# A fused decoder layer: the cross-head scores in blocks of two tokens (64x32 pieces of TensorE's array), picked from two candidates in place of four

## What is computed

```python
q = (query @ Wq.T + bq).reshape(b, s, 16, 64)      # query: x after sublayer 1
k = (key @ Wk.T + bk).reshape(b, s, 16, 64)        # key, value: ctx
scores = jnp.einsum('bshd,bsgd->bshg', q, k) / 8   # head h against head g of the SAME token
attn = softmax(scores, axis=-1)
out = jnp.einsum('bshg,bsgd->bshd', attn, v)
```

## Time and profile before

| | |
|---|---|
| three runs | 489.27, 483.74, 486.50 us; median 486.5 |
| the profiled execution | 491.25 us, of which 489.4 us from the first to the last instruction |
| TensorE's mean granted clock | 0.972 |
| busy | PE 426.4 us, PEld 364.3, DVE 342.6, ACT 242.7, POOL 146.5 |

### The profile page before, as it was taken

The page is one execution under the profiler, slowest core; times in us unless marked ns, Lnnn a source line. Parts: engine busy times, 40 slices in busy tenths (PEclk is TensorE's granted clock), DMA queues, the critical chain, the costliest instruction groups (busy, mean ns, idle before and its releaser), DMA issues.

```text
span 489.4 us, 12635 instructions
## 1 busy us (share of the span) xinstructions
PE 426.4 (87%) x4788; PEld 364.3 (74%) x4788; DVE 342.6 (70%) x751; ACT 242.7 (50%) x828; POOL 146.5 (30%) x218
## 2 busy tenths in 40 slices
PE   8779699999898977999898977899898989999793
PEld 7568577778787866778787866778787877778683
DVE  2543788884958794884958794875958798967534
ACT  3584646534565353534565353643565364645431
POOL 5030425050330533050321542151321543512121
PEclk9889899999999997999999997999999999999998
DMA  8800201110100112010100112010100110101002
GB/s 214 308 2 1 50 7 45 55 40 2 29 23 12 40 26 70 13 38 1 30 23 12 39 27 68 17 35 5 29 18 16 37 29 21 43 6 43 21 1 64
DMA packets 43588, 19.10 MB, mean 39 GB/s; under 512 B 36544, under 2 KB 40896, under 8 KB 43536
## 3 DMA queue, kind: packets, MB, share of 16 engines
q1 hardware_dynamic: 42688, 16.88, 12.5%
q0 software_dynamic: 560, 1.38, 1.1%
q10 hardware_dynamic: 288, 0.07, 0.1%
HBM read 8.88 MB, written 1.05 MB: 20 GB/s over the span
## 4 chain that ended last, share of the span: by engine, by line
PE 61%; DVE 21%; issue 9%; ACT 4%; POOL 3%; DMA 2%; SPq 0%; POOLq 0%; DVEq 0%; ACTq 0%
PE ps L1018 7%; PE ps L923 6%; PE ps L1096 6%; PE ps L1071 6%; PE ps L948 6%; DVE pt L660 4%; DVE qt L705 4%; PE ps L1196 3%; PE ps L903 3%; PE ps L972 3%; PE ps L905 3%; PE ps L1135 3%; PE ps L904 3%; DVE ot L643 3%; DVE neg_max L712 3%
## 5 line engine op out<-in xcount | busy, mean ns | idle before, releaser
L496 ACT ACTIVATE p<-ps,neg_max 128x128 f32<-128x128 f32 x256 | 91.1, 414 | 66.9 <-DVE neg_max L712 66.9
L386 POOL TENSOR_TENSOR p<-p,row_inv 128x1024 f32<-128x1024 f32 x32 | 60.4, 1898 | 104.1 <-DVE row_inv L794 97.1
L489 ACT ACTIVATE pt<-ps 128x512 f32<-128x512 f32 x64 | 34.9, 607 | 66.6 <-PE ps L1018 66.5
L496 ACT ACTIVATION_READ_ACCUMULATOR p<-ps,neg_max 128x1 f32 x256 | 65.3, 255 | 0.0
L705 DVE TENSOR_TENSOR qt<-ps,bq 64x256 f32<-64x256 f32 x128 | 53.4, 417 | 7.5 <-PE ps L1135 5.8
L1018 PE MATMUL ps<-ident,p 128*128 128x128 f32 x256 | 37.2, 300 | 10.3 <-issue 7.1
L712 DVE TENSOR_REDUCE neg_max<-ps 128x4 f32<-128x512 f32 x64 | 42.1, 683 | 0.2 <-PE ps L1122 0.2
L1018 PEld LDWEIGHTS ps<-ident,p 128*128 128x128 f32 x256 | 31.7, 154 | 13.8 <-issue 11.5
L1135 PE MATMUL ps<-x1t,wq 128*128 128x128 f32 x256 | 36.5, 286 | 5.8 <-DVE pt L660 3.0
L948 PE MATMUL ps<-wo,ot 128*128 128x128 f32 x256 | 32.3, 279 | 10.0 <-DVE ot L643 10.0
L1135 PEld LDWEIGHTS ps<-x1t,wq 128*128 128x128 f32 x256 | 31.1, 191 | 11.8 <-DVE pt L660 8.1
(11 more groups left out here) (138 smaller groups left out, 891.7 us busy)
## 6 DMA issues: line engine op xcount, KB each, us to landing
v<-v2s SPq DMA_DIRECT2D x256, 32.0 KB
xg<-x_t SPq DMA_DIRECT2D x4, 256.0 KB, 2.7
pt<-w_qk SPq DMA_DIRECT2D x4, 256.0 KB, 7.2
cg<-ctx_t SPq DMA_DIRECT2D x4, 256.0 KB, 3.1
wo<-w_o SPq DMA_DIRECT2D x2, 512.0 KB, 9.1
out<-x2b SPq DMA_DIRECT2D x4, 256.0 KB, 2.3
xres<-x_nat SPq DMA_DIRECT2D x15, 64.0 KB, 1.7
bv_row<-b_v POOLq DMA_DIRECT2D x1, 512.0 KB, 10.7
```

What stands on the lines that cost most here:

```text
L386: nc.gpsimd.tensor_tensor(ph, ph, row_inv[:, 8 * half:8 * half + 8].unsqueeze(2).to_broadcast([T, 8, T]), ALU.mult).then_inc(p_ready, 1)
L496: last = nc.scalar.activation(p[:, hd * T:(hd + 1) * T], bank(S_BANK[q])[:, pos * T:(pos + 1) * T], ACT.Exp, bias=neg_max[:, hd:hd + 1], a ...
```

## The change

It cuts the tokens of a product from four to two. The constant `JB` = 2 is new. Each round i now has two blocks `ja` of two tokens for each half: 64 products of 64x32 in a step in place of 32 of 64x64. A block's stationary and moving operands are 32 columns each, and its result goes to partitions 64*pp + 32*ja on, so that a product occupies an eighth of the array (rows 64*ih, columns 64*pp + 32*ja), given as `tile_position`. The products' results fill the first 32 of every 64 columns of the PSUM banks. The pick takes two candidates: one `tensor_scalar` and one `scalar_tensor_tensor`. `own_j` has two columns and is made for `% JB` on the host.

```diff
-        own_j = sb("own_j", [128, J])
+        own_j = sb("own_j", [128, JB])
...
-                    scores = bank(S2, BANK, 2).rearrange("p (i j g) -> p i j g", i=IH * K, j=J)
+                    scores = bank(S2, BANK, 2).rearrange("p (i x j g) -> p i x j g", i=IH * K, x=2, j=JB)[:, :, 0]
                     own = s2v
                     nc.vector.tensor_scalar(own, scores[:, :, 0], own_j[:, 0:1], None, ALU.mult).then_inc(own_picked, 1)
-                    for j in range(1, J):
-
-                        dve.wait_ge(own_picked, (J - 1) * s - (J - 1) + j)
-                        nc.vector.scalar_tensor_tensor(out=own, in0=scores[:, :, j], scalar=own_j[:, j:j + 1], in1=own,
-                                                       op0=ALU.mult, op1=ALU.add).then_inc(own_picked if j < J - 1 else s2_ready, 1)
+                    dve.wait_ge(own_picked, s)
+                    nc.vector.scalar_tensor_tensor(out=own, in0=scores[:, :, 1], scalar=own_j[:, 1:2], in1=own,
+                                                   op0=ALU.mult, op1=ALU.add).then_inc(s2_ready, 1)
                     max2(s + 1)
...
                     for i in range(K * 2):
                         k, pp = i // 2, i % 2
-                        first = ((phase - 1) % GB * K * 2 + i) * J * H
-                        for ih in range(IH):
-                            rows = slice(64 * ih, 64 * ih + 64)
-                            last = nc.tensor.matmul(bank(S2 + ih)[64 * pp:64 * pp + 64, k * 64:(k + 1) * 64],
-                                                    qt2[rows, i * J * H:(i + 1) * J * H], kb[rows, first:first + J * H], start=True, stop=True)
+                        for ja in range(J // JB):
+                            own = i * J * H + ja * JB * H
+                            first = (phase - 1) % GB * HALF * H + own
+                            below = 64 * pp + 32 * ja
+                            for ih in range(IH):
+                                rows = slice(64 * ih, 64 * ih + 64)
+                                last = nc.tensor.matmul(bank(S2 + ih)[below:below + 32, k * 64:k * 64 + 32],
+                                                        qt2[rows, own:own + JB * H], kb[rows, first:first + JB * H], start=True, stop=True,
+                                                        tile_position=(64 * ih, below))
                     last.then_inc(mm_s2, 1)
```

More of the change, by code:

```diff
@@ L39 @@
 IH, J, K = 2, 4, 8
+JB = 2
 FH, FL = 512, 64
@@ L1269 @@
     mask[np.arange(128), np.arange(128) // H] = 1.0
-    own_j = np.zeros((128, J), np.float32)
-    own_j[np.arange(128), np.arange(128) // H % J] = 1.0
+    own_j = np.zeros((128, JB), np.float32)
+    own_j[np.arange(128), np.arange(128) // H % JB] = 1.0
     x = np.asarray(x)
```

## The result

Four runs of the changed kernel have a median of 499.81 us (496.76 to 502.47), four of the kernel before 487.88 (483.74 to 489.52): a ratio (of the means) of 1.0256, with an interval of [1.0164, 1.0347]. The forecast was 485.7 us, no change, and its range ended at 497.0. The profiled execution of after took 500.1 us, its span is 498.3, against 491.25 and 489.4 before; TensorE's mean granted clock is 0.976 (before 0.972).

What follows compares the result with a forecast made beforehand. TensorE was taken as the bound from the output projection 948 through the next one. Products 0, step 1 -0.4, pick -0.9 and instructions +0.5 sum to -0.8 us, giving 485.7 us from the median 486.5; 8-in-10 range 481.0 to 497.0.

Steps and rivals of the forecast that it cites:

- Where the change stands: TensorE's cross-head scores lie on the path in every step, VectorE's pick in hardly any.
- The products: count and price: Scores in each step: 128 records at 6.8 ns plus 0.22 us fixed make 1.09 us, no change.
- four pieces streaming 32 columns: Scores: the array work per product halves on four pieces, 6.8 ns per record, paying exactly for twice the products.
- the row of the starts: Scores: narrow windows show four records starting within 0.03 us, at most one each 7.5 ns, 1.18 us per set.
- the pace is per record, not per column: Rival: a record takes about 13.6 ns whatever its size, scores 1.96 us, kernel 499.6 us; chance 0.22.
- More instructions: TensorE's 2,048 added instructions make late fetches at the loop's branch likelier: +0.5 us (0 to +7.1).
- the fetches bind: Rival: both idle times at the branch double, +7.1 us, kernel 492.3 us; chance 0.05.
- The pick: VectorE's shorter pick gains 0.23 us from step 15 into 16 and 0.66 behind step 16: -0.9 us (0 to -2.0).
- in an ordinary step: VectorE waits for others soon behind the pick, so its 1.0 us saved per step counts zero.
- Step 1: Its scores, 1.99 us at the lower clock, were to change by -0.4 us (0 to -0.9).
- The sum: Whole kernel: 0 - 0.4 - 0.9 + 0.5 = -0.8 us, 485.7 us from the median of 486.5.
- signs that the forecast had named: Scores of 1.4 us or more, 0.8 or less, releaserless TensorE idle inside or behind them, or steps a microsecond shorter.

Runs made afterwards that it cites:

- e7_half: Changed kernel with only the first block of each round, 32 products of 64x32 (half of the scores left out): 480.65 us, 0.9856 of the kernel before.
- e13_one_pass: Changed kernel with qt2 and kb in bfloat16, each product one load and one matmul: 486.14 us, 0.9977 of the kernel before.
- e2_products_only: Changed kernel with its 64 products of 64x32 but four picks again, two of them times zero: 499.9 us, 1.0242 of the kernel before.
- e1_pick_only: Kernel before with its 32 products of 64x64, but VectorE picks only two of four candidates: 485.15 us against 487.45, 0.9951.
- e5_moving16: Changed kernel with 16 moving columns in place of 32, same number of instructions: 501.15 us, 1.0264 of the kernel before.
- e6_moving64: Changed kernel with 64 moving columns in place of 32, same number of instructions: 502.42 us, 1.0289 of the kernel before.
- e8_twice: Kernel before with each of its 64x64 products made twice, 128 records per set of scores: 505.69 us, 1.0357 of the kernel before.
- e9_after_shift80: Changed kernel with 20 short matmuls behind TensorE's warm-up, later instructions 80 places further on: 504.88 us, 1.032 of the kernel before.
- e11_after_shift128: Changed kernel with 32 short matmuls behind TensorE's warm-up, later instructions 128 places further on: 507.56 us, 1.0427 of the kernel before.
- e3_after_shift128: Changed kernel with 128 increments of an unused semaphore at the head of TensorE's program: 515.26 us, 1.057 of the kernel before.
- e10_before_shift80: Kernel before with 20 short matmuls behind TensorE's warm-up, 80 instructions: 493.2 us, 1.0097 of the kernel before.
- e4_before_shift128: Kernel before with 128 increments of an unused semaphore at the head of TensorE's program: 505.87 us, 1.0379 of the kernel before.

## Why the prediction was wrong, point by point

- **Where the change stands** was right: the scores lie on the path in every step, the pick in hardly any.
- **"The products: count and price"** is the step that failed. The count, 128 records, was right. The price of 6.8 ns per record came from "four pieces streaming 32 columns" and from the row of the starts. But the runs with 16 and 32 columns show that streaming is no bound there, and a burst of four starts says nothing of a run of 128. The windows of after, L1198 alone, show how a burst misleads (the first figure behind x is the matmul records in flight):

```profile
134.56:134.73 0.17, 0.17 (x32) 0.17 (x33) 1.00 0.44 107
134.73:134.80 0.07, 0.07 (x32) 0.07 (x18) 1.00 0.30 62
```

  The first 32 records start within 0.17 us, some 5.2 ns apart, faster even than forecast. In the next 0.07 us none is added. From then on the trace has a product each 16.7 ns, which is 8.4 ns per record, with a pause of some 0.2 us near the 90th; over the block it is 1.44/128 = 11.3 ns. In the blocks of 1.64 to 1.76 us the pauses add up to 0.3 to 0.45 us. Over the 13 steps they come to 3.4 of the 6.0 us. Their cause is open: no run here moves them by design, and e7_half and e13_one_pass, with half of the instructions, have none in step 4. The forecast 1.09 us were 1.44 to 1.76, +6.0 us in 13 steps and some 0.7 of the 1.74 in steps 6 and 10, where the sum had 0.
- **The rival "the pace is per record, not per column"** had the mechanism for the changed kernel and was dear by a seventh of its price: 11.7 ns per further record and not 13.6. Its point of decision, 10 ns, was passed. That its total, 499.6 us, lies 0.2 from the measured 499.81 is luck: it had 1.96 us per set of scores, which took 1.44 to 1.76, and no stops, which made up for it. It also had the 13.6 ns of the kernel before as a pace of records, and e7_half's 0.69 us for as many records say that there it was not. It was weighed at 0.22 because the earlier trace rows seemed to speak for streaming: at the lower clock the same block took 1.99 us. That is a reading of 64x64 products, whose size counts (1.09 us against e7_half's 0.69 for as many records); it doesn't carry over to 64x32.
- **"More instructions"** was far too small: +0.5 us, for the branches alone. Behind steps 4, 8 and 12 it is +4.25 us, in the scores of step 1 a stop of 2.28 us, and at the branches 8.2 us of idle time for 7.1. This is the second step that failed. "Nothing in the chain before shows one in a straight stretch" was true and no argument: before, a set of scores used up 128 instructions in 1.1 us, now it uses up 256, as many as a packet holds. The rival "the fetches bind" looked for it at the branches, where little of it was.
- **"The pick"**: -0.9 us forecast. 0.23 and 0.66 us were right in kind: line 1095 of step 16 and line 929 behind it wait no longer, and the 1.28 us for ScalarE's gelu stay, as the timeline of after shows:

```profile
438.24 1.95 PE L1095 MATMUL ps<-wo,ot 128*128 128x128 f32 x16
...
463.64 1.16 PE L971 MATMUL ps<-wdn,qt 128*128 128x128 f32 x8 [1.28 <-ACT qt L482]
465.35 0.44 PE L929 MATMUL ps<-ident,p 128*128 128x128 f32 x2
```

  These places gave 0.49 and 0.79 us, and 0.6 more came by the wait for `x` (line 773), which the step "in an ordinary step" had put at zero. -1.9 us in all.
- **Step 1** gave nothing of the -0.4 us: its scores took 2.11 us more, for the stop of 2.28 us inside them. In e2_products_only, which has no stop there, they take 0.16 us less than before.
- **The sum**: -0.8 was forecast. With the measured terms it is +6.0 + 1.7 + 4.3 + 3.0 - 2.2 - 1.9 - 2.1 = +8.8, the 8.9 us between the two spans but for rounding. The medians are 11.9 us apart, with an interval that holds both.

Two of the signs that the forecast had named for its being wrong came together: scores of 1.4 us or more, and idle times without a releaser inside and behind them.

No version here with the whole computation is faster than the kernel before. e1_pick_only and e7_half leave out part of it, e13_one_pass changes its numbers.

## What to carry to other kernels

The long row of tiny products here was priced by its instructions: count loads and matmuls, and take the pace from a run as long as the one that is planned, never from a burst of four. Cutting a product into two halves can pay only as long as the array's work is the bound; where it no longer is, the halves cost together more than the whole did (1.44 us for 1.09). And whoever puts as many instructions as one fetch brings into less time than a fetch takes should look for idle time without a releaser, not in that place but a little behind it.

## What the runs showed of the hardware

**Fetches of instructions.** 0.82 MB in 50 packets are 16.4 KB each; the Trainium skill (Runtime: NRT & Kernel Launch, Instruction fetch mechanics) says that they come in blocks of 16 KiB, 256 instructions, and the packets' size agrees. Such a packet lies right ahead of the stop of step 4. Queues of after from 135.5 to 137.0 us (neither the 0.9 us before nor the 1.4 behind have one of q8):

```profile
q8 instruction: 1, 0.02, 6.0%
```

6.0% of 16 engines' 1.5 us is the 1.44 us which it took, from 135.52 to 136.96 by its own record; the engine went on at 138.45, 1.5 us behind its landing. It is so at all the other stops of after, e2_products_only, e5_moving16, e6_moving64, e8_twice, e9_after_shift80, e11_after_shift128 and e3_after_shift128: inside or behind the scores TensorE goes on 1.2 to 1.6 us behind the landing of a q8 packet, which took 0.9 to 1.5 us. Where the packet has landed ahead of the scores there is no stop: in steps 3, 7 and 11 of after it lands 0.5 to 0.7 us before they begin. And it settles step 1. In after, no q8 packet moves from 50 us to the start of the scores at 54.38, and one comes inside them (55.34 to 56.60). In e2_products_only one had landed by 51.6, and its scores, from 54.91 on, run through. Queues of e2_products_only from 50.5 to 52.0 us:

```profile
q8 instruction: 1, 0.02, 3.7%
```

Where the stops come can be counted in TensorE's list of instructions, in blocks of 256. The count takes a load or a matmul as one instruction each, and has 16 instructions ahead of the program's own, which is an assumption:

| kernel, step | scores begin at | instructions from there to the stop | stop at |
|---|---|---|---|
| after, 4 | 179 | 256 + 2x15 | 465 |
| after, 1 | 246 | 2x110 | 466 |
| e9_after_shift80, 6 | 235 | 2x116 | 467 |
| e11_after_shift128, 2 | 220 | 2x123 | 466 |

That all four stop at the same place of a block, within two instructions, doesn't depend on the 16; where the borders lie does. By this count they stop some 46 instructions short of 512, the second border behind the scores' start: the engine runs through the first and is held at the same distance ahead of the next. The picture that fits is that the fetch is asked for near one border and must have landed by the time that the engine is so close to the next. From the record at the first border to the going on it is some 3.6 us in after's step 4, 3.7 in e9_after_shift80 and 3.4 in e11_after_shift128. No run shows what sets the 46, and the place alone doesn't decide: steps 3, 7 and 11 of after begin at 240 and step 1 of e2_products_only at 246, and neither stops, since their packets came early. The same page of the Trainium skill says that crossing a border is mostly hidden, since the sequencer is slower than the fetch, at some 20 cycles per instruction. The rows here disagree for these products: four instructions in 16.7 ns, and stops of up to 2.6 us.

**The branch** costs more, the fewer instructions have passed since the last border (one trace for each place). The longest idle time is 3.3 us with 236 instructions since it (e10_before_shift80), 3.8 with 156 (before), 4.5 with 28 (e4_before_shift128); with the 64x32 products it is 3.7, 4.1 and 4.9 (e9_after_shift80, after, e3_after_shift128). The waits of e10_before_shift80 and of e4_before_shift128:

```profile
PE ps L1021 <- issue: 6.5, 2, 3.3
```

```profile
PE ps L1022 <- issue: 8.7, 2, 4.5
```

The packets of the queue go with it. From the start of step 6's scores to the going on, the queues of before (182.0 to 186.9 us) and of after (186.1 to 191.6) have:

```profile
q8 instruction: 1, 0.02, 1.8%
```

```profile
q8 instruction: 2, 0.03, 3.1%
```

At the two branches of before the only packet took 1.39 and 0.95 us. In after the second one starts within 0.11 us of the first one's landing and takes 1.58 and 1.65. In e3_after_shift128 the two overlap, and the second takes 1.98 and 2.07. TensorE goes on 1.5 to 1.6 us behind its landing in the first two, 1.8 and 2.0 in the last. So the fetch for the branch was slower in the runs where another one ran beside it or just ahead of it.

**The pace of TensorE.** The fastest row of float32 loads and matmuls seen is 32 records some 5.2 ns apart, then 8.4 ns each with pauses; with 16 moving columns it is hardly faster than with 32 (1.41 us for 1.44). That the sequencer sets this pace is a reading: the runs show 4.2 ns per instruction, whatever the columns and the type. A counted-up semaphore costs TensorE 0.16 us.
